# Second-stage transposes one more piece ahead, those of blocks 4 to 6 some chunks of look-ups later

## The chip, the cores and the metric

The kernel runs on one core of a Trainium2 chip. The time is the device time of one execution in microseconds (us), lower is better; times shown are medians over runs.

## What is computed

The reference is the interaction tower of a recommendation model. For each of 512 samples it looks up one 128-wide row in each of 26 tables, takes all pairwise dot products of these rows and of the rows with a dense vector, and sends the result through three layers:

```python
e = jnp.stack([tbl_f[ids[:, f]] for f in range(26)], axis=1)      # 512 x 26 x 128
sd = jnp.einsum('bfd,bd->bf', e, dense)
ss = jnp.einsum('bfd,bgd->bfg', e, e)
pairs = ss[:, iu, ju]                                             # f < g
h = concat([dense, sd, pairs, dense], axis=1)                     # 512 x 607
h = relu(h @ W_top1 + b_top1)                                     # 512
h = relu(h @ W_top2 + b_top2)                                     # 256
y = h @ W_top3
```

## The kernel before, in words

All arithmetic is in float32. The five engines run programs of their own, written out by hand; each is a fixed order of instructions with waits on counting semaphores, so the order in which the kernel's text issues work is the order of execution.

**Where the rows come from.** Ten of the tables have 1000 rows each. They are read whole, and TensorE picks their rows with one-hot matrices (line 342, "look-ups"). The other sixteen tables are gathered: GpSimd (POOL) issues 64 indirect DMAs (line 294), each of 128 rows of 512 bytes. Four of them make one block of 32 samples; there are 16 blocks, b0 to b15. The ring `rows` holds three blocks, so the gathers of block n wait until block n - 3 has been transposed by TensorE (semaphore `staged`), and POOL takes the blocks strictly in order.

**Look-ups.** Six groups g = 0 to 5 of one or two tables, with eight chunks k = 0 to 7 each. A chunk is two matmuls per table, and counts up `chunk_done`. VectorE makes the one-hot matrix of a chunk (line 552) into a ring of eight, so that of chunk m waits until chunk m - 8 is done; ScalarE moves a finished group into the tile `ET` (lines 480 and 482).

**Second-stage transposes.** A block is transposed by TensorE with four matmuls (line 325) into one of two PSUM banks `stage`, and ScalarE copies the bank into `ET` (line 470, `empty_stage`), which counts up `stage_taken`. Two banks mean that the transposes of a block wait until the block but one before them has been copied. Where they stand is set by three tables of names: `AMID` (behind chunk k of group g of the look-ups), `SOON` (directly behind the Gram matrices of piece p, ahead of that piece's layers) and `LATER` (behind the layers of piece p).

**Pieces.** The samples are then taken in nine pieces, p = 0 to 6 of 64 samples (two blocks) and p = 7 and 8 of 32. For each piece TensorE computes a Gram matrix per sample, 64 small matmuls of 27 columns in groups of four (line 371; the trace holds two records for each, 128 per piece of 64 samples), then the transposes of `SOON`, then the layers that are due for earlier pieces (lines 387, 398, 413, 415), then the transposes of `LATER`. The Gram matrices of piece p read blocks 2p and 2p + 1 (pieces 7 and 8: b14 and b15). VectorE and ScalarE move each Gram bank into the tile `Z` (lines 568 and 492), VectorE folds it (579, 586), and both take the first layer's output out of PSUM (591 and 501).

On TensorE the order behind the look-ups is `gram_piece(p)`, `SOON[p]`, `layers(p)`, `LATER[p]`. `layers(0)` and `layers(1)` are empty, `layers(2)` holds half of the first layer of 128 samples, and those from `layers(3)` on parts of both first layers.

Of the kernel before, what the change touches and what calls it, by code (L numbers as in the profile page):

```python
# [56 lines left out]
def layer1_of(p):  # L57

    return [((p - 2) // 2, c) for c in ((2, 3) if p % 2 else (0, 1))] if 2 <= p < NP - 1 else []
# [47 lines left out]
def dlrm_tower(nc, x, out):  # L107
    ctx = ExitStack()
    with ctx:
# [6 lines left out]
        def sem(name):  # L116
# [81 lines left out]


        AMID = {(0, 7): ["dense"], (1, 3): ["b0"], (2, 1): ["b1"], (2, 5): ["b2"], (3, 1): ["b3"],  # L200
                (3, 6): ["b4"], (4, 3): ["b5"], (4, 7): ["b6"], (5, 7): ["b7"]}

        SOON = {1: ["b8"], 2: ["b9"], 3: ["b10"], 4: ["b11"], 5: ["b12"]}
        LATER = {5: ["b13"], 6: ["b14"], 7: ["b15"]}
        STAGED = [s for g, k in sorted(AMID) for s in AMID[g, k]] + [s for n in range(NP) for s in SOON.get(n, []) + LATER.get(n, [])]

        def bank_of(name):
# [101 lines left out]
        def _(pe):  # L309
            def transposes(name):  # L310


                before, bank = STAGED.index(name), bank_of(name)
                if before >= 2:
                    pe.wait_ge(stage_taken, before - 1)
                if name == "dense":
                    pe.wait_ge(ident_ready, 1)
                    pe.wait_ge(dense_in, 16)
                    for t in range(T):
                        last = pe.transpose(bank[:, P * t:P * (t + 1)], dense_rows[:, t, :], ident[:, :])  # L320
                else:
                    n = int(name[1:])
                    pe.wait_ge(gathered[n], 16 * GB)
                    for k in range(GB):
                        last = pe.transpose(bank[:, P * k:P * (k + 1)], rows[:, (GB * n + k) % ROWS_RING, :], ident[:, :])  # L325
                last.then_inc(staged, 1)
# [37 lines left out]
            def gram_piece(p):  # L364

                gram_ready(p)
                b0, size = PIECES[p]
                for j in range(size // 4):
                    for i in range(4):
                        b = b0 + 4 * j + i  # L370
                        last = pe.matmul(gram[p % 2][32 * i:32 * i + 32, NV * j:NV * (j + 1)], ET[:, VP * b:VP * (b + 1)],  # L371
                                         ETv[:, b, 0:NV], start=True, stop=True)
                last.then_inc(gram_done, 1)
# [45 lines left out]
            def layers(p):  # L419

                for t, c in layer2_of(p):
                    layer2(t, c)
                for t, c in layer1_of(p):
                    layer1_dense(t, c)
                    layer1(t, c)
# [3 lines left out]
            for p in range(NP):  # L429
                gram_piece(p)  # L430
                for name in SOON.get(p, ()):
                    transposes(name)
                layers(p)
                for name in LATER.get(p, ()):
                    transposes(name)
# [13 lines left out]
        def _(act):  # L449
# [11 lines left out]
            def empty_stage(name):  # L461

                act.wait_ge(*filled(name))
                bank = bank_of(name)
                if name == "dense":
                    act.copy(denseT[:, :], bank[:, :])
                    act.copy(ETv[:, :, DENSE], bank[:, :]).then_inc(stage_taken, 1)
                else:
                    n = int(name[1:])
                    act.copy(ETv[:, BS * n:BS * (n + 1), 0:NM],  # L470
                             bank[:, :].rearrange("d (b v) -> d b v", v=NM)).then_inc(stage_taken, 1)
# [12 lines left out]
            def move_gram(p):  # L484
# [5 lines left out]
                for i in (2, 3):  # L490
                    for dst, src in z_moves(p, (i,)):
                        last = act.copy(dst, src)  # L492
                    if i == 2:
                        for name in SOON.get(p, ()):
                            empty_stage(name)
                last.then_inc(gram_act, 1)

            def take_odd(t, c):

                act.wait_ge(h1_done, HC * t + c + 1)  # L500
                act.activation(h1T[:, t % 2, c, :], layer1_bank(t, c), ACT.Relu, bias=b1c[:, c:c + 1]).then_inc(h1_odd, 1)  # L501
# [31 lines left out]
            for p in range(NP):  # L533
                move_gram(p)
                if layer1_of(p):
                    take_odd(*layer1_of(p)[1])
                for name in LATER.get(p, ()):
                    empty_stage(name)
# [152 lines left out]
```

## Time and profile before

| | |
|---|---|
| runs of the kernel before | 131.85, 132.18, 134.35 us |
| median | 132.18 us |
| the profiled execution's time | 132.72 us |
| its span in the trace | 130.9 us |
| TensorE busy | 94.0 us, 72% |
| VectorE, ScalarE, GpSimd busy | 73.7, 61.8, 67.5 us |
| granted TensorE clock, mean | 0.896 |

The span is the part of the execution that the trace covers; 1.8 us lie around it. The page of the profile gives busy times and, in 40 slices, how busy each engine was. The timeline lists an engine's instructions in order of time, merged where they follow each other without a gap, with the idle time before them and its inferred releaser in brackets. "issue" is idle time for which the profile shows no semaphore as the cause.

### The profile page before, as it was taken

To read this page: it belongs to the slowest core of one execution; us is meant where nothing else is said; L and a number is where in the kernel's file an instruction comes from. 1 tells how busy PE (TensorE), PEld (TensorE's weight loads), DVE (VectorE), ACT (ScalarE), POOL (GpSimd) and SP (SyncE) were. 2 spreads that over 40 slices of the span, in tenths; PEclk is the share of its full clock that TensorE was granted. 3 is DMA by queue.
4 is the path that set the end of the run, shared out by engine and by line. 5 is a ranking of instruction groups with operands and counts; after the bars stand their busy time and mean duration, and the time that the engine had idled before them with its cause. 6 is when DMAs were issued, how large, how long until landed. Compare 5 with 4: busy or idle time off the path is not lost.

```text
span 130.9 us, 3331 instructions
## 1 busy us (share of the span) xinstructions
PE 94.0 (72%) x1420; PEld 78.2 (60%) x1420; DVE 73.7 (56%) x170; ACT 61.8 (47%) x131; POOL 67.5 (52%) x70
## 2 busy tenths in 40 slices
PE   0089899999969999000547459397784997897892
PEld 0157688888858887000436349286674796786780
DVE  1387999999997835000008927264370731974621
ACT  3435591966908506300308909164370904964410
POOL 2878888787888787770831725538172560000000
PEclk9999999999999999965557756999999559999999
DMA  2999965947996121220110110102011110000000
GB/s 53 242 379 367 272 242 185 267 115 179 381 372 207 44 60 40 63 59 21 44 41 8 45 40 25 49 16 60 25 38 43 25 40 25 0 5 0 8 0 1
DMA packets 6849, 13.37 MB, mean 102 GB/s; under 512 B 2353, under 2 KB 3506, under 8 KB 6834
## 3 DMA queue, kind: packets, MB, share of 16 engines
q1 hardware_dynamic: 4112, 8.95, 21.4%
q0 software_dynamic: 2048, 4.20, 11.2%
q8 instruction: 11, 0.18, 0.6%
q10 hardware_dynamic: 674, 0.01, 0.3%
q14 instruction: 4, 0.03, 0.1%
HBM read 13.15 MB, written 0.00 MB: 100 GB/s over the span
## 4 chain that ended last, share of the span: by engine, by line
PE 44%; POOL 17%; issue 15%; DMA 7%; another core or an unknown queue 6%; ACT 6%; DVE 2%; DVEq 0%; ACTq 0%
POOL rows L294 17%; PE gram L371 12%; PE hidden L398 8%; PE second L415 6%; PE gram L342 6%; DMA rows<-in_tables_gather,idx 5%; PE stage L325 5%; PE hidden L387 3%; PE hidden L342 2%; ACT Z L492 2%; ACT ET L470 2%; ACT ET L482 2%; PE second L413 2%; DVE Z L568 2%
## 5 line engine op out<-in xcount | busy, mean ns | idle before, releaser
L294 POOL DMA_INDIRECT rows<-in_tables_gather,idx x64 | 66.8, 1044 | 39.0 <-issue 17.4
L568 DVE COPY Z<-gram 32x112 f32<-32x112 f32 (+3 forms) x72 | 23.0, 320 | 35.5 <-PE gram L371 34.6
L371 PE MATMUL gram<-ET 128*32 128x27 f32 x1024 | 17.0, 207 | 25.8 <-issue 12.8
L492 ACT COPY Z<-gram 32x112 f32<-32x112 f32 (+1 forms) x72 | 23.2, 322 | 23.7 <-PE gram L371 22.9
L371 PEld LDWEIGHTS gram<-ET 128*32 128x32 f32 x1024 | 14.1, 123 | 29.4 <-issue 26.0
L552 DVE TENSOR_SCALAR onehot<-ids,rowid 128x1024 fp32r<-128x1024 int16 (+1 forms) x48 | 28.7, 659 | 5.1 <-DMA ids<-in_ids_one 2.1
L342 PE MATMUL gram<-onehot,part 128*128 128x512 f32 x80 | 22.5, 434 | 6.6 <-DVE part L558 6.2
L342 PEld LDWEIGHTS gram<-onehot,part 128*128 128x128 f32 x80 | 16.4, 211 | 10.7 <-DVE onehot L552 6.2
L342 PE MATMUL hidden<-onehot,part 128*128 128x512 f32 x80 | 19.7, 397 | 0.6 <-issue 0.6
L342 PEld LDWEIGHTS hidden<-onehot,part 128*128 128x128 f32 x80 | 14.6, 188 | 3.7 <-issue 0.8
L558 DVE TENSOR_TENSOR part<-raw,part 128x1024 fp32r<-128x1024 f32 (+2 forms) x11 | 12.1, 1123 | 3.1 <-issue 2.4
L398 PE MATMUL hidden<-Z,W1s 128*128 128x128 f32 x84 | 13.2, 301 | 0.6 <-DVE Z L579 0.6
L398 PEld LDWEIGHTS hidden<-Z,W1s 128*128 128x128 f32 x84 | 12.2, 219 | 0.8 <-DVE Z L579 0.8
L459 ACT CAST part<-raw 128x1024 fp32r<-128x1024 f32 x9 | 9.4, 1070 | 5.2 <-DMA raw<-in_tables_one 4.3
L470 ACT COPY ET<-stage 128x512 f32<-128x512 f32 x16 | 9.5, 592 | 4.8 <-issue 4.6
L325 PE MATMUL stage<-ident,rows 128*128 128x128 f32 x64 | 10.8, 295 | 1.0 <-DMA rows<-in_tables_gather,idx 1.0
L415 PE MATMUL second<-W2s,h1T 128*128 128x256 f32 x32 | 10.2, 436 | 0.0
L325 PEld LDWEIGHTS stage<-ident,rows 128*128 128x128 f32 x64 | 8.0, 150 | 2.5 <-issue 1.4
L482 ACT COPY ET<-gram 128x512 f32<-128x512 f32 x5 | 5.3, 1145 | 6.9 <-PE hidden L342 5.6
L415 PEld LDWEIGHTS second<-W2s,h1T 128*128 128x128 f32 x32 | 5.8, 206 | 1.6 <-ACT h1T L501 0.4
L501 ACT ACTIVATE h1T<-hidden,b1c 128x128 f32<-128x128 f32 x7 | 2.6, 367 | 7.3 <-PE hidden L398 7.2
L387 PE MATMUL hidden<-denseT,W1e 128*128 128x128 f32 x28 | 6.0, 306 | 0.0
(38 smaller groups left out, 42.2 us busy)
## 6 DMA issues: line engine op xcount, KB each, us to landing
raw<-in_tables_one SPq DMA_DIRECT2D x9, 512.0 KB
ids<-in_ids_one SPq DMA_DIRECT2D x4, 256.0 KB, 5.5
rows<-in_tables_gather,idx POOLq DMA_INDIRECT x64
W1s<-in_W_pairs SPq DMA_DIRECT2D x1, 768.0 KB
W1d<-in_W_dense SPq DMA_DIRECT2D x1, 512.0 KB
W2s<-in_W_top SPq DMA_DIRECT2D x1, 512.0 KB
raw<-in_tables_one SPq DMA_DIRECT2D x1, 384.0 KB
ids<-in_ids_one SPq DMA_DIRECT2D x2, 128.0 KB, 3.6
```

The costliest lines, as they stand in the source:

```text
L294: pool.indirect_dma_start(out=rows[:, m % ROWS_RING, :], out_offset=None, in_=x["tables_gather"], in_offset=bass.IndirectOffsetOnAxis(ap=i ...
L325: last = pe.transpose(bank[:, P * k:P * (k + 1)], rows[:, (GB * n + k) % ROWS_RING, :], ident[:, :])
L342: last = pe.matmul(look_banks(g)[j], part[:, i % 4, n, D * k:D * (k + 1)], onehot[:, (KR * g + k) % RING, B * j:B * (j + 1)], start=(k == ...
L371: last = pe.matmul(gram[p % 2][32 * i:32 * i + 32, NV * j:NV * (j + 1)], ET[:, VP * b:VP * (b + 1)], ETv[:, b, 0:NV], start=True, stop=True)
L387: pe.matmul(layer1_bank(t, c), W1e[:, P * c:P * (c + 1)], denseT[:, P * t:P * (t + 1)], start=True, stop=False)
L398: last = pe.matmul(layer1_bank(t, c), W1s[:, s, P * c:P * (c + 1)], Z[:, t % ZT, s, :], start=False, stop=(s == 0))
L415: last = pe.matmul(at, h1T[:, t % 2, c, :], W2s[:, c, :], start=False, stop=(c == HC - 1))
L470: act.copy(ETv[:, BS * n:BS * (n + 1), 0:NM], bank[:, :].rearrange("d (b v) -> d b v", v=NM)).then_inc(stage_taken, 1)
L492: last = act.copy(dst, src)
L552: dve.tensor_scalar(onehot[:, m % RING, 0:w], ids16[:, B * SIDE[g][0]:B * SIDE[g][0] + w], rowid[:, k:k + 1], None, ALU.is_equal).then_inc ...
L558: return dve.tensor_tensor(part[:, i % 4, 1, cols], raw[:, i % RAW, cols], part[:, i % 4, 0, cols].bitcast(F32), ALU.subtract)
L568: last = dve.tensor_copy(dst, src)
```

## The change

Two tables of names change, and nothing else; no instruction is added or taken away.

```diff
         AMID = {(0, 7): ["dense"], (1, 3): ["b0"], (2, 1): ["b1"], (2, 5): ["b2"], (3, 1): ["b3"],
-                (3, 6): ["b4"], (4, 3): ["b5"], (4, 7): ["b6"], (5, 7): ["b7"]}
-
-        SOON = {1: ["b8"], 2: ["b9"], 3: ["b10"], 4: ["b11"], 5: ["b12"]}
-        LATER = {5: ["b13"], 6: ["b14"], 7: ["b15"]}
+                (4, 1): ["b4"], (4, 4): ["b5"], (5, 1): ["b6"], (5, 7): ["b7"]}
+
+        SOON = {p: [f"b{p + 8}"] for p in range(6)}
+        LATER = {6: ["b14"], 7: ["b15"]}
```

So b8 moves from behind piece 1 to behind piece 0, and so on up to b12, which moves from piece 5 to piece 4. b13 moves from behind the layers of piece 5 to ahead of them. In the look-ups b4 moves three chunks later, b5 one and b6 two; b7 stays. The gathers stand in the same order on GpSimd, but wait for transposes that stand elsewhere: those of b11 wait for b8, and so on to b15, which waits for b12.

On TensorE, at the first pieces behind the look-ups (`gram` is the bank of the Gram matrices, `stage` that of the transposes, and the number behind `gathered` is the block):

```order
 L371 MATMUL gram<-ET 32x27 [waits et_again,look_taken,stage_taken]
 L371 MATMUL gram<-ET 32x27 x63
+L325 MATMUL stage<-ident,rows 128x128 [waits gathered8,stage_taken]
+L325 MATMUL stage<-ident,rows 128x128 x3
 L371 MATMUL gram<-ET 32x27 [waits stage_taken]
 L371 MATMUL gram<-ET 32x27 x63
-L325 MATMUL stage<-ident,rows 128x128 [waits gathered8,stage_taken]
+L325 MATMUL stage<-ident,rows 128x128 [waits gathered9,stage_taken]
 L325 MATMUL stage<-ident,rows 128x128 x3
 L371 MATMUL gram<-ET 32x27 [waits gram_act,gram_dve,look_taken,stage_taken]
 L371 MATMUL gram<-ET 32x27 x63
```

The transposes of b8 now stand between the Gram matrices of pieces 0 and 1, and those of b9 where those of b8 stood.

On TensorE, at the end of the layers of piece 5, ahead of the Gram matrices of piece 6:

```order
 L387 MATMUL hidden<-denseT,W1e 128x128 [waits h1_odd]
 L398 MATMUL hidden<-Z,W1s 128x128 x3
-L325 MATMUL stage<-ident,rows 128x128 [waits gathered13,stage_taken]
-L325 MATMUL stage<-ident,rows 128x128 x3
 L371 MATMUL gram<-ET 32x27 [waits gram_dve,gram_act,stage_taken]
 L371 MATMUL gram<-ET 32x27 x63
```

The Gram matrices of piece 6 now follow the layers of piece 5 directly.

On TensorE, at the end of group 3 of the look-ups and the start of group 4:

```order
 L342 MATMUL hidden<-onehot,part 128x512 [waits onehot_ready]
 L342 MATMUL hidden<-onehot,part 128x512 x3
+L342 MATMUL hidden<-onehot,part 128x512 [waits onehot_ready]
+L342 MATMUL hidden<-onehot,part 128x512 x3
+L342 MATMUL gram<-onehot,part 128x512 [waits lo_ready,onehot_ready,look_taken]
+L342 MATMUL gram<-onehot,part 128x512
+L342 MATMUL gram<-onehot,part 128x512 [waits lo_ready]
+L342 MATMUL gram<-onehot,part 128x512
+L342 MATMUL gram<-onehot,part 128x512 [waits onehot_ready]
+L342 MATMUL gram<-onehot,part 128x512 x3
 L325 MATMUL stage<-ident,rows 128x128 [waits gathered4,stage_taken]
 L325 MATMUL stage<-ident,rows 128x128 x3
```

Three chunks that stood behind the transposes of b4 now stand ahead of them.

## Rows read from the trace of the kernel before

**Rows 1.** The page: TensorE's busy tenths and granted clock in 40 slices
```profile
PE   0089899999969999000547459397784997897892
PEclk9999999999999999965557756999999559999999
```
**Rows 2.** Chain that ended last, at the hole: start, us, what
```profile
53.65 8.20 another core or an unknown queue
...
61.87 0.38 ACT ET L480
```
**Rows 3.** Timeline of TensorE from 62 us: start, us, what, xcount, idle before
```profile
62.35 0.85 PE L371 MATMUL gram<-ET 128*32 128x27 f32 x46 [10.01 <-ACT ET L480]
67.84 2.72 PE L371 MATMUL gram<-ET 128*32 128x27 f32 x189 [1.12 <-issue]
70.49 0.65 PE L325 MATMUL stage<-ident,rows 128*128 128x128 f32 x4
72.09 0.87 PE L371 MATMUL gram<-ET 128*32 128x27 f32 x47 [0.95 <-ACT Z L492]
77.09 1.21 PE L371 MATMUL gram<-ET 128*32 128x27 f32 x71 [0.51 <-issue]
78.23 1.12 PE L325 MATMUL stage<-ident,rows 128*128 128x128 f32 x4
...
85.28 0.92 PE L371 MATMUL gram<-ET 128*32 128x27 f32 x82 [1.15 <-issue]
...
92.75 0.97 PE L371 MATMUL gram<-ET 128*32 128x27 f32 x89 [0.53 <-issue]
...
100.29 1.01 PE L371 MATMUL gram<-ET 128*32 128x27 f32 x87 [1.20 <-issue]
```
**Rows 4.** Timeline of GpSimd: gathers of b9 to b12 and b15, first or last
```profile
54.48 0.94 POOL L294 DMA_INDIRECT rows<-in_tables_gather,idx  x1 [0.30 <-issue]
...
62.17 0.94 POOL L294 DMA_INDIRECT rows<-in_tables_gather,idx  x1 [3.00 <-remote]
...
65.91 0.94 POOL L294 DMA_INDIRECT rows<-in_tables_gather,idx  x1 [0.31 <-issue]
71.41 0.94 POOL L294 DMA_INDIRECT rows<-in_tables_gather,idx  x1 [4.56 <-PE stage L325]
...
83.36 0.95 POOL L294 DMA_INDIRECT rows<-in_tables_gather,idx  x1 [0.30 <-issue]
...
106.37 0.94 POOL L294 DMA_INDIRECT rows<-in_tables_gather,idx  x1 [0.31 <-issue]
```
**Rows 5.** Chain that ended last: transposes of b9 to b13, a layer, piece 6
```profile
78.30 1.05 PE stage L325 x4
...
86.20 0.59 PE stage L325 x4
86.79 0.43 PE second L413 x2
...
89.39 0.67 PE hidden L398 x6
...
93.71 0.59 PE stage L325 x4
...
101.30 1.05 PE stage L325 x4
...
108.25 0.45 PE stage L325 x4
...
109.36 1.29 PE gram L371 x83
```
**Rows 6.** Timeline of TensorE in the look-ups: transposes of b4, group 5
```profile
38.49 0.63 PE L325 MATMUL stage<-ident,rows 128*128 128x128 f32 x4 [1.03 <-DMA rows<-in_tables_gather,idx]
...
47.98 3.92 PE L342 MATMUL hidden<-onehot,part 128*128 128x512 f32 x16
```
**Rows 7.** Timeline of VectorE: the last one-hot matrix
```profile
50.38 0.49 DVE L552 TENSOR_SCALAR onehot<-ids,rowid 128x512 fp32r<-128x512 int16 x1 [0.94 <-PE hidden L342]
```

## Prediction

> **What bounds the kernel now.** I read the page's slices first. TensorE is close to full up to about 52 us, then empty for three slices, and from 62 us on half busy with a pattern that repeats [rows 1]. So there are three stages, and the change touches the first and the last. Next the chain that ended last: through the hole it shows 8.20 us in which ScalarE waits for the end of the look-ups, with no releaser that the trace can name [rows 2]. Then the timelines of TensorE and GpSimd from 62 us on, laid side by side. The reader should see this in them: piece 0 starts at 62.35, issues 46 of its records in 0.85 us, and then crawls until 67.84, when the rest of pieces 0 and 1 goes through without a gap, 189 records in 2.72 us [rows 3]. The four gathers of b10 run from 62.17 to 66.85, which is 65.91 + 0.94 [rows 4]. The crawl ends 0.99 us behind them. Piece 2 does the same: 47 records, a crawl, and the rest from 77.09; b11's gathers start at 71.41 and take the same 4.68 us, so they end at 76.09, 1.00 earlier [rows 3, 4]. Piece 3 resumes at 85.28, and b12's gathers end at 84.31, 0.97 earlier [rows 3, 4]. Pieces 4 and 5 resume at 92.75 and 100.29 in the same way [rows 3]. Piece 6 meets no gather (the last one ends at 106.37 + 0.94 = 107.31, it starts at 109.36) and goes through in 1.29 us [rows 4, 5]. Piece 1 meets none either.
>
> So the last stage is bound by a loop that no share of busy time shows: transposes of block n let the gathers of block n + 3 go; while these run, the Gram matrices of the piece behind them stall once some 46 records have been issued; the stall ends about 1.0 us after the last gather; the rest of the piece and the next transposes follow. From the end of b9's transposes (78.30 + 1.05 = 79.35) to that of b10's (86.79) the loop takes 7.44 us, to b11's (94.30) 7.51, to b12's (102.35) 8.05 [rows 5]. The layers of each piece lie inside the loop, ahead of the Gram matrices, and are covered by the gathers.
>
> **The change part by part.** It moves transposes only; what counts is how many blocks of gathers a Gram piece has to sit out. Behind 62 us six blocks are still to be gathered, b10 to b15, in both kernels. Before, five of them stall a piece (0, 2, 3, 4, 5), and b15's run beside the layers of piece 5. After, b8's transposes stand behind piece 0, so b11's gathers start under piece 1, which ran free before, and b15's under piece 5: six pieces stall, 0 to 5.
>
> The sum, from the moment at which b7's transposes count as done, 61.85 (ScalarE's wait ends then, 53.65 + 8.20 [rows 2], and GpSimd's first gather follows at 62.17 [rows 4]):
>
> - Look-ups. b4's transposes waited 1.03 us for their gathers [rows 6]; three chunks later they find them landed, and all behind moves up 1.0. Whether the hole moves with it is unknown: VectorE's last one-hot matrix waits for the last chunk of group 4 and is released at 50.38 only, after 0.94 us of idling, although group 5 was running on TensorE from 47.98 on [rows 6, 7]. The counts arrive late, and the trace does not say why. Bounds: 0 gained if the hole's end is fixed by something else, 1.4 gained if one count fewer is queued, and 1.4 lost if b5's and b6's counts queue too. I take 1.0 gained, since the late counts follow chunks: start at 60.85. b5 and b6 move without cost: they sit between chunks either way, and the gathers of b8 and b9 that wait for them start after them still (b9's first at 54.48 [rows 4], well behind chunk 1 of group 5).
> - To b8's end: the stall of piece 0 ends at 67.84, 5.99 behind 61.85. In the chain the rest of piece 0 takes 1.10. b8's transposes now run in the low clock: 1.05 as b9's did [rows 5], where b8's took 0.65 [rows 3]. 5.99 + 1.10 + 1.05 = 8.14, so 68.99.
> - To b9's end, the new stall: 0.27 to the first gather (b8's end 71.14 to 71.41), 4.68 for four gathers, 1.0 to the end of the stall, the rest of the piece, 1.05 of transposes. Piece 1 starts together with the gathers and not 0.7 behind them as piece 2 did, so a little more of it is through; I take 0.9 for its rest, between 0.7 and the 1.21 of piece 2 [rows 3]. Together 7.9: 76.9.
> - To b10's end the same, piece 2 now: 7.9, bounds 7.44 and 8.2: 84.8.
> - To b11, b12 and b13: three turns of the loop with layers in it, as before. 7.44 + 7.51 + 7.6 (the third is 8.05 less the 0.46 by which transposes in the high clock are shorter [rows 5]) = 22.55: 107.35.
> - The layers of piece 5. In the high clock those of piece 3, which are the same instructions, took from 86.79 to 90.06 (89.39 + 0.67), 3.27 [rows 5]; before, piece 5's stood in a stretch in which the clock was granted at half (slices 32 and 33 [rows 1]) and took 5.90, from 102.35 to 108.25 [rows 5]. I take 3.27: 110.6.
> - Piece 6 follows at once. Before, b13's transposes and ScalarE's copy of them took 1.11, from 108.25 to 109.36 [rows 5]. That cost is gone, and is already left out of the sum.
>
> Piece 6 starts at 110.6 where it started at 109.36: 1.25 later. Behind it nothing changes. The profiled execution becomes 132.72 + 1.25 = 133.97, and since it lay 0.54 above the median, I expect 133.4. A stretch of half clock over piece 5's layers, as before, costs 0.46 + 2.63 more: 136.5.
>
> ScalarE's copies are hidden: b8's moves into its work on piece 0, b13's into that on piece 5, each 0.58 behind four moves out of the Gram bank, with the next user more than 2 us away.
>
> One rule against the trace. A piece under gathers loses over 4 us between its first 46 records and its rest [rows 3, 4]. The Trainium skill, page "SBUF — State Buffer", section "SBUF: two separate sides", says that DMA and TensorE use separate ports and cannot slow each other. By it the stall would have nothing to do with the gathers' data, moving them would cost nothing, and the sum would be rival C's, 130.1. What the trace shows is only that five stalls end within 0.97 to 1.04 us of the end of a block of gathers; it does not show by what way.
>
> **The rivals.**
> - A, my forecast: piece 1 stalls. For it: the 46 and 47 records that pieces 0 and 2 issue whatever the lead of the gathers (0.18 and 0.68 us). Something holds about that many ahead and is not refilled under gathers. Piece 1 has 128. Time 133.4, or with the half clock over the layers 136.5.
> - B: the gathers bite only once their data moves, and piece 1 is through by then (it lasts 1.3 to 1.55 us). Against it: piece 0 stalled at 63.20, 0.09 us after its first gather's issue ended. Then b9's end comes at about 71.5, the gathers of b11 and b12 run back to back (eight at 1.25 us from 69.3), piece 2 sits both out until 79.9, and b10 ends at 81.6 instead of 84.8: 3.2 less, 130.2, or 133.3 with the half clock.
> - C, the other side: the gaps belong to the pieces and not to the gathers, their ends a coincidence of two loops locked to each other. Then piece 1 stays free and every piece keeps its length; the change saves the 1.0 in the look-ups and the 1.11 ahead of piece 6: 132.18 - 2.1 = 130.1, and 127.0 if the half clock over piece 5's layers is gone too. It decides if piece 1 runs through under b11's gathers without a gap and piece 2 does not make up for it. Against it: five ends of five in step with the gathers, and pieces 1, 6, 7 and 8, without gathers, without a gap. The rule of the page above speaks for this one.
> - D: the hole grows, because the late counts queue behind those of b5 and b6: A plus up to 2.4, 135.8.
>
> **How the numbers follow.** A with the high clock over piece 5's layers 0.40, A with the low clock 0.28 (the page shows the low level in two stretches behind 56 us, one of them just there; a stretch starts in or behind a stall, and six stalls give it as many chances), B 0.14, C 0.13, D 0.05. The likeliest, 133.4, is the forecast. The range reaches from B and C to A with the low clock: 130.1 to 136.6. About 2% can be told from no change, so 129.5 to 134.8 is "the same". Faster: half of C where the clock gains too, 0.07. Slower: A with the low clock, D and a little of A by the bounds of its turns: 0.35. The rest, 0.58, is the same.
>
> **What would show it.** In the profile of the changed kernel: a gap inside piece 1's Gram matrices that ends about 1.0 us after b11's last gather; b15's gathers before the end of piece 5 and a gap there too; 7.4 to 8.2 us between the ends of transposes b8 to b13; no wait at b4's transposes, and the end of the hole near 60.9; piece 6 straight behind the layers of piece 5 at 110.6, or 113.7 in the low clock. If piece 1 has no gap, A is wrong. If the hole ends at 61.9 or later, the gain of the look-ups is not there.

## The result, and the profile after

The changed kernel took 137.18 us (median of 4 runs, 135.34 to 138.85), the kernel before beside it 132.3 us. The ratio of the two is 1.029, with an interval of 1.016 to 1.042 (it leaves out disturbed runs, and so lies below the 1.037 of the medians). In a second set of runs it was 1.039 (1.028 to 1.049). So the change makes the kernel some 3 to 4% slower. The forecast was 133.4 us with a range up to 136.6. The median lies 0.6 us above the range; the ratio times 132.18 us gives 136.0.

The profiled execution took 137.69 us, its span is 135.9. The page's slices of the changed kernel, TensorE and its granted clock:

```profile
PE   0089799999999991212394755929987799988893
PEclk9999999999999999755555555797799757999999
```

Against [rows 1] the half clock lasts longer: from slice 18 to 25 without a break, and again in slice 33, with 0.7 in the slices beside it. The timeline of TensorE in the changed kernel (start, us, what, xcount, idle before):

```profile
51.25 0.63 PE L325 MATMUL stage<-ident,rows 128*128 128x128 f32 x4 [0.39 <-issue]
56.69 0.63 PE L371 MATMUL gram<-ET 128*32 128x27 f32 x28 [4.80 <-issue]
...
67.49 1.39 PE L371 MATMUL gram<-ET 128*32 128x27 f32 x83 [0.50 <-issue]
68.81 1.12 PE L325 MATMUL stage<-ident,rows 128*128 128x128 f32 x4
69.85 1.22 PE L371 MATMUL gram<-ET 128*32 128x27 f32 x51
71.48 0.33 PE L371 MATMUL gram<-ET 128*32 128x27 f32 x4 [0.41 <-issue]
...
75.82 1.00 PE L371 MATMUL gram<-ET 128*32 128x27 f32 x56 [0.51 <-issue]
76.75 1.12 PE L325 MATMUL stage<-ident,rows 128*128 128x128 f32 x4
77.79 1.23 PE L371 MATMUL gram<-ET 128*32 128x27 f32 x51
...
83.77 1.04 PE L371 MATMUL gram<-ET 128*32 128x27 f32 x58 [1.10 <-issue]
```

Piece 1, which had no gap before [rows 3], issues 51 records from 69.85 on, crawls from 71.1 to 75.82, and issues its last 56 then. Piece 2 does the same 7.94 us later. GpSimd's timeline of the changed kernel shows b11's gathers, first and last:

```profile
70.19 0.94 POOL L294 DMA_INDIRECT rows<-in_tables_gather,idx  x1 [4.82 <-PE stage L325]
...
73.95 0.94 POOL L294 DMA_INDIRECT rows<-in_tables_gather,idx  x1 [0.30 <-issue]
```

They end at 74.89, 0.93 ahead of the end of the crawl. The chain that ended last, in the changed kernel, shows the ends of the transposes and the layers of piece 5 (those of before are [rows 5]):

```profile
68.87 1.05 PE stage L325 x4
...
76.81 1.05 PE stage L325 x4
...
84.81 1.05 PE stage L325 x4
...
92.62 0.59 PE stage L325 x4
...
100.04 0.59 PE stage L325 x4
...
107.65 1.05 PE stage L325 x4
108.69 0.72 PE second L413 x2
109.42 2.00 PE second L415 x4
...
114.41 1.22 PE gram L371 x82
```

Piece 6 starts at 114.41 where it started at 109.36: 5.05 later, and the span grew by 5.0. All of the loss lies ahead of piece 6, as forecast.

### The profile page after: what moved, and what is told of

Same layout as the page of the kernel before. It is cut to its first block, busy times and chain, and to the rows that moved or that the text cites. A ratio compares the mean times of both kernels' runs of the same rounds, so it can differ in the third digit from the quotient of the medians.

```text
span 135.9 us, 3331 instructions
## 1 busy us (share of the span) xinstructions
PE 99.5 (73%) x1420; PEld 81.4 (60%) x1420; DVE 73.5 (54%) x170; ACT 61.9 (46%) x131; POOL 67.7 (50%) x70
## 4 chain that ended last, share of the span: by engine, by line
PE 67%; issue 20%; DMA 5%; DVE 3%; ACT 2%; SPq 2%; DVEq 0%
PE gram L371 15%; PE hidden L342 14%; PE gram L342 11%; PE hidden L398 8%; PE stage L325 7%; PE second L415 7%; DMA raw<-in_tables_one 5%; PE hidden L387 3%; PE second L413 2%; ACT part L459 2%; DVE Z L568 1%; PE stage L398 1%; ACT ET L470 1%; SPq L258 1%; DVE onehot L552 1%
## 5 line engine op out<-in xcount | busy, mean ns | idle before, releaser
L371 PE MATMUL gram<-ET 128*32 128x27 f32 x1024 | 21.1, 211 | 25.2 <-issue 23.7
L371 PEld LDWEIGHTS gram<-ET 128*32 128x32 f32 x1024 | 16.3, 126 | 30.8 <-issue 28.5
L325 PE MATMUL stage<-ident,rows 128*128 128x128 f32 x64 | 11.8, 314 | 0.4 <-issue 0.4
L415 PE MATMUL second<-W2s,h1T 128*128 128x256 f32 x32 | 11.2, 469 | 0.0
L325 PEld LDWEIGHTS stage<-ident,rows 128*128 128x128 f32 x64 | 8.5, 159 | 2.0 <-issue 0.8
L415 PEld LDWEIGHTS second<-W2s,h1T 128*128 128x128 f32 x32 | 6.3, 223 | 1.8 <-issue 0.5
L482 ACT COPY ET<-hidden 128x512 f32<-128x512 f32 x4 | 4.2, 1174 | 5.5 <-PE hidden L342 5.5
```

Source lines behind the costliest of these rows:

```text
L415: last = pe.matmul(at, h1T[:, t % 2, c, :], W2s[:, c, :], start=False, stop=(c == HC - 1))
```

## The experiments

The kernel before took 131 to 134 us in some sets of runs and 107 to 111 us in others, and chip 8 showed both (109.4 us in one set, 132.0 us in a later one). Within one set it kept to one of the two. I call them the crawling and the quiet condition, after what their traces show below; no trace says what makes the difference. Each kernel is compared with the kernel before of its own set. Some kernels were run again because their first run had fallen in the quiet condition.

### Before and after once more

The kernel before again, for its trace: 

> The kernel before, unchanged, for its trace on the chip of the experiments, where it took 109.4 us and not 132.2. Theory G (on this chip no Gram piece crawls under gathers; GpSimd issues without a pause and its gathers' landing is what TensorE waits for): pieces 0 and 1 go through back to back without a gap, b8's transposes wait 1 to 2 us for their gathers, and GpSimd's gathers stand 1.25 us apart up to the last. Rival (the crawl is there too, shorter): gaps with releaser issue of over 1 us in at least three pieces.

It fell in the crawling condition, on chip 10: 133.21 us. Its timeline of TensorE:

```profile
52.31 0.55 PE L371 MATMUL gram<-ET 128*32 128x27 f32 x41
53.17 0.26 PE L371 MATMUL gram<-ET 128*32 128x27 f32 x4 [0.32 <-issue]
...
67.41 2.65 PE L371 MATMUL gram<-ET 128*32 128x27 f32 x178 [0.50 <-issue]
```

The theory for the quiet condition could not be tried here. But the trace shows that the hole of [rows 2] is no stage of its own. In this execution piece 0 starts at 52.31, right behind the look-ups, and crawls until 67.41: 15 us for its first 78 records, under the gathers of b8, b9 and b10, which run without a pause to 65.12. Whether piece 0 starts at 52.3 or at 62.35 [rows 3], its rest comes at 67.4 to 67.8.

The changed kernel again: 

> The changed kernel, unchanged, on the chip of the experiments. The two halves alone gave ratios 0.989 (look-ups) and 1.031 (pieces). Theory G: the halves add, ratio 1.015 to 1.025, with waits for gathers at b8's, b9's and b10's transposes of 6 to 8 us in all. Rival (the pieces' half costs more when the look-ups end earlier, since the gathers land no earlier): the look-ups' gain is eaten by longer waits, ratio 1.025 to 1.035, waits of 8 us or more.

Measured in the crawling condition: ratio 1.039 (1.028 to 1.049). Both expectations were for the other condition, so neither could be tried. Its trace (an execution of 136.98 us) has the same loop, with the end of b8's transposes at 69.16 and that of b13's at 107.35. Two rows of its chain that ended last, b13's transposes and piece 6:

```profile
106.71 0.64 PE stage L325 x4
...
113.50 1.42 PE gram L371 x94
```

From the end of b13's transposes to piece 6 it takes 6.15 us, the layers of piece 5.

### Each half alone

```diff
# look-ups' half: AMID of after, SOON and LATER of before
# pieces' half: AMID of before, SOON and LATER of after
```

The look-ups' half: 

> The look-ups' half of the change alone: b4, b5 and b6 later, the pieces as before. Theory A (the pieces' half costs, the look-ups' half gains a little): b4's transposes wait no more (1.03 us), but the end of b10's gathers moves up by some 0.4 us only, as in the changed kernel, where the rest of piece 0 started at 67.49 and not 67.84; time 0.3 to 1.0 us below before, ratio 0.992 to 0.998. Rival (the look-ups' half costs, because the counts of b5, b6 and b7 reach the other engines later): the rest of piece 0 starts later than 67.84 and the time is above before.

The pieces' half: 

> The pieces' half alone: b8 behind piece 0 and so on, the look-ups as before. Theory A (one more block of gathers sits inside a Gram piece): nearly the whole loss, ratio 1.025 to 1.045 (4 to 5.5 us), gaps in pieces 0 to 5, piece 6 starts at 114 to 115. Rival (the loss comes from the look-ups' half or from both together): ratio within 0.99 to 1.01.

Both fell in the quiet condition. The look-ups' half gave 0.989 (0.983 to 0.995), the pieces' half 1.031 (1.017 to 1.044). The repeat of the look-ups' half fell there too (chip 7): 

> The look-ups' half alone once more. On chip 8 it gave a ratio of 0.989. Where the pieces crawl, the start of the pieces is set by the end of b10's gathers (67.4 to 67.8 in the traces of before and after), and b4's missing wait of 1.03 us moves the start of b10's gathers only as far as b7's transposes move: theory A expects 0.990 to 1.000; rival (the look-ups' half carries part of the 1.03 to 1.04 that the whole change costs): 1.005 to 1.015.

It gave 0.997 (0.991 to 1.002). So in the quiet condition the look-ups' half gains between nothing and 1.7%, and the pieces' half is what costs. In the crawling condition neither half was timed alone. The way in which the pieces' half costs is another one here, and the gaps and the start of piece 6 that I had expected of it are not there. The pieces' half, quiet condition, timeline of TensorE:

```profile
52.27 1.83 PE L371 MATMUL gram<-ET 128*32 128x27 f32 x128
57.29 1.09 PE L325 MATMUL stage<-ident,rows 128*128 128x128 f32 x4 [3.19 <-DMA rows<-in_tables_gather,idx]
58.31 2.20 PE L371 MATMUL gram<-ET 128*32 128x27 f32 x128
61.65 1.08 PE L325 MATMUL stage<-ident,rows 128*128 128x128 f32 x4 [1.14 <-DMA rows<-in_tables_gather,idx]
62.66 2.03 PE L371 MATMUL gram<-ET 128*32 128x27 f32 x128
66.66 1.08 PE L325 MATMUL stage<-ident,rows 128*128 128x128 f32 x4 [1.97 <-DMA rows<-in_tables_gather,idx]
```

No piece crawls. TensorE reaches piece 0 with its clock high and finishes it in 1.83 us, and then waits 3.19, 1.14 and 1.97 us for b8, b9 and b10 to land. In the look-ups' half, where b8 stands behind piece 1, the same engine's timeline has

```profile
55.23 1.67 PE L371 MATMUL gram<-ET 128*32 128x27 f32 x109 [1.45 <-issue]
56.83 0.66 PE L325 MATMUL stage<-ident,rows 128*128 128x128 f32 x4
...
62.19 1.09 PE L325 MATMUL stage<-ident,rows 128*128 128x128 f32 x4 [1.66 <-DMA rows<-in_tables_gather,idx]
```

b8's transposes wait for nothing, and only b9's wait, 1.66 us. Its piece 6 starts at 84.26, that of the pieces' half at 86.56. In the quiet condition GpSimd issues one gather each 1.25 us with hardly a wait, so blocks land at a rate that TensorE can't hasten; asking for b8 to b10 one piece earlier turns into waiting. From b11 on the transposes wait for no gather in either trace.

### The gathers held back from piece 1

```diff
                 pool.wait_ge(*filled(...))
+                if n == 11 and k == 0:
+                    pool.wait_ge(gram_done, 2)
```

Tried three times. The first two fell in the quiet condition, where b11's gathers (from 64.09 on) come long after piece 1 anyway, so the added wait does nothing there. One run each gave 110.46 us beside 109.36 and 109.83 us beside 108.36: ratios 1.010 and 1.014. They stand in for the changed kernel itself, which was not timed in the quiet condition. Single runs of the kernel before reached 110.61 and 109.84 us in the same two sets, so what the whole change costs there is not clear of noise. The second and the third: 

> The changed kernel with b11's gathers held until piece 1's Gram matrices are done, once more, because the first try ran on chip 8, where no piece crawls. On a chip where they do (before takes 132 us): theory A: piece 1 goes through without a gap, 128 records in 1.3 to 1.6 us; b11's and b12's gathers run back to back and piece 2 crawls under all eight of them; b10's transposes end 1.5 to 3 us earlier than in the changed kernel there. Rival: piece 1 has a gap of 4 us all the same.

 

> The changed kernel with b11's gathers held until piece 1's Gram matrices are done, now timed. On a chip like chip 8, where no piece crawls, the held gathers come some 6 us after that moment anyway, so the kernel stands for the changed kernel itself: ratio to before 1.010 to 1.025. On a chip like chip 10 theory A expects that piece 1, if piece 0's rest starts at 67.4 to 67.8, goes through without a gap (128 records in 1.3 to 1.6 us), that piece 2 crawls under b11's and b12's eight gathers, and a ratio of 1.00 to 1.03, below that of the changed kernel there (1.039). Rival: piece 1 has its gap of 4 us all the same, and the ratio is 1.04 or more.

The third fell in the crawling condition, on chip 8. Its timeline of TensorE:

```profile
67.26 1.41 PE L373 MATMUL gram<-ET 128*32 128x27 f32 x85 [0.50 <-issue]
68.60 1.12 PE L327 MATMUL stage<-ident,rows 128*128 128x128 f32 x4
69.64 1.93 PE L373 MATMUL gram<-ET 128*32 128x27 f32 x128
71.50 0.78 PE L327 MATMUL stage<-ident,rows 128*128 128x128 f32 x4
72.46 0.85 PE L373 MATMUL gram<-ET 128*32 128x27 f32 x48 [0.17 <-issue]
...
83.78 0.85 PE L373 MATMUL gram<-ET 128*32 128x27 f32 x43 [0.50 <-issue]
84.56 1.12 PE L327 MATMUL stage<-ident,rows 128*128 128x128 f32 x4
```

and that of GpSimd, first and last of the eight gathers of b11 and b12:

```profile
72.38 1.09 POOL L296 DMA_INDIRECT rows<-in_tables_gather,idx  x1 [8.18 <-PE stage L327]
...
81.29 0.95 POOL L296 DMA_INDIRECT rows<-in_tables_gather,idx  x1 [0.31 <-issue]
```

Piece 1 goes through without a gap, 128 records in 1.93 us (granted clock 0.50; I had expected 1.3 to 1.6), at the same place in the program where it crawled in the changed kernel. That shows the cause of its crawl: the gathers that run beside it, and not its place. Piece 2 then crawls under all eight, up to 83.78. The ratio is 1.041 (1.034 to 1.049), no better than the changed kernel's 1.039, where I had expected 1.00 to 1.03. My expectation of 1.5 to 3 us gained at b10's transposes missed too: b10's transposes end at 85.7, in the changed kernel at 84.81 + 1.05 = 85.9. From b11's first gather to b10's end it takes 13.3 us here (72.38 to 85.68) and 15.7 in the changed kernel (70.19 to 85.86): 2.4 saved, but the gathers began 2.2 later. What piece 1 saves by missing its block of gathers, piece 2 pays.

### A longer ring

```diff
-ROWS_RING = 3 * GB
+ROWS_RING = 7 * GB
```

on top of the look-ups' half, so that the gathers hardly wait for transposes: 

> The look-ups' half of the change, pieces as before, and a ring for seven blocks in place of three, so that the gathers of block n wait for the transposes of block n - 7. Theory G (on this chip GpSimd never waits for the ring): nothing moves against the look-ups' half alone, ratio to before 0.985 to 0.995. Where a Gram piece crawls under gathers (the chip of the first runs, 132 us), theory A expects the gathers to run through and to end near 85 us, pieces 0 and 1 to crawl up to there, and the pieces behind them to go free: 4 to 8 us less than before.

Measured in the crawling condition: 143.74 us, ratio 1.085 (1.076 to 1.094). I expected 4 to 8 us less than before, and it was 11 us more. TensorE's timeline:

```profile
53.56 0.44 PE L371 MATMUL gram<-ET 128*32 128x27 f32 x28 [0.70 <-issue]
...
76.22 0.20 PE L371 MATMUL gram<-ET 128*32 128x27 f32 x1 [2.59 <-issue]
79.02 0.20 PE L371 MATMUL gram<-ET 128*32 128x27 f32 x1 [2.60 <-issue]
...
90.92 2.92 PE L371 MATMUL gram<-ET 128*32 128x27 f32 x200 [0.50 <-issue]
```

This trace is of the slowest of the five executions (146.43 us). GpSimd's last gather of the run without a pause, in its timeline:

```profile
84.59 0.95 POOL L294 DMA_INDIRECT rows<-in_tables_gather,idx  x1 [0.30 <-issue]
```

It ends at 85.54. Piece 0 crawls for 37 us, from 53.56 to 90.92, at times with one record in 2.8 us. So the crawl lasts as long as the gathers are let run, whatever the reason for which they run; it also gets slower with their number, and its tail, the time from the end of the last gather to the end of the crawl, grows: 0.93 us behind four gathers (changed kernel, b11), 2.3 behind the three blocks before 65.12 (before, second trace), 5.4 behind this run. That is why my expectation for this kernel failed. I had the gathers' end right (85), but not the tail, and only 28 records of piece 0 get done in the crawl, so that 200 records of pieces 0 and 1 stand behind it. And b15's gathers, which wait for b8's transposes even in this ring, run from 95.15 to 99.94 and make piece 2 crawl once more; only pieces 3 to 5 go free.

### Gathers left out, and plain DMAs in their place

```diff
-            for n in range(NB):
+            for n in range(10):
                 for k in range(GB):
                     gather(n, k)
```

> The changed kernel without the gathers of b10 to b15, and without TensorE's waits for them: these blocks are transposed from the rows that lie in the ring, so the results for samples 320 to 511 are not those of the reference, and 24 of 64 gathers are left out. Theory A: pieces 0 to 5 lose their gaps; the time from the first record of piece 0 to that of piece 6 falls from 57.6 us to 24 to 30 us, and with the end of b9's gathers near 59.5 us piece 0 goes through by 61 to 62; whole time 98 to 106 us. Rival (the gaps belong to TensorE's own issue): gaps of 3 us or more stay in at least three pieces and the time stays above 120 us.

And with the six blocks brought by plain DMAs from SyncE:

```diff
+            for n in range(10, NB):
+                sp.wait_ge(*filled(f"b{n - 3}"))
+                for k in range(GB):
+                    m = GB * n + k
+                    sp.dma_start(rows[:, m % ROWS_RING, :], x["tables_gather"][P * m:P * (m + 1), :]) ...
```

> The changed kernel with the gathers of b10 to b15 replaced by plain DMAs of the same size (128 rows of 512 bytes that lie one behind the other) issued from SyncE's queue behind the same waits: samples 320 to 511 are computed from other rows. The same bytes land in the same tiles. Where the pieces crawl: if the data in flight makes them crawl, gaps in pieces 1 to 5 stay, shorter since four transfers take less time. If GpSimd's making of the gathers does, there is no gap from piece 1 on and the time falls to within 2 us of the kernel that leaves them out.

Both (and the repeat of the first) fell in the quiet condition, one run each, so they say nothing of the crawl, and neither expectation on it could be tried. Leaving 24 of 64 gathers out brought 108.16 us beside 109.36 and 106.31 beside 108.36, a ratio of 0.989 and 0.981; the plain DMAs 107.87 beside 108.36. One thing is to be read from them. Piece 5's Gram matrices, in the pieces' half, in the repeat without late gathers, and with plain DMAs, each a row of TensorE's timeline:

```profile
80.92 1.85 PE L371 MATMUL gram<-ET 128*32 128x27 f32 x128
```
```profile
77.14 1.29 PE L372 MATMUL gram<-ET 128*32 128x27 f32 x128
```
```profile
78.33 1.29 PE L377 MATMUL gram<-ET 128*32 128x27 f32 x128
```

The granted clock was 1.00 over all three. In the windows of the last, data came in at 104 GB/s over that very piece (78.3 to 79.6); over the first, where gathers run, it was 53. So in the quiet condition too a Gram piece is slowed by GpSimd's gathers, by 0.56 us or 43%, and not by data in flight. The plain DMAs were not run in the crawling condition; that the same holds for the crawl is not shown. The rule that I had weighed (the Trainium skill, page "SBUF — State Buffer", section "SBUF: two separate sides": a DMA cannot be slowed by a compute operation nor the other way round) agrees with the plain DMAs' 1.29 us. It doesn't account for the 1.85 us under gathers. The crawl, which the longer ring and the held gathers tie to the gathers, goes against the reading that gathers cost TensorE nothing.

## Why the prediction was right, and where it was off

The change makes the kernel slower, where the prediction had put 0.58 on "the same" and 0.35 on "slower". The loop, the sixth stall and the new stall of piece 1 came as forecast; one term of the sum, the layers of piece 5, had the wrong size.

**Right: the bound.** The loop of gathers, crawl, rest and transposes sets the time up to piece 6, in both kernels, in the crawling condition. Two kernels show by intervention that the gathers hold the pieces back: gathers held until piece 1 was done freed piece 1, and gathers let run kept piece 0 back until 90.9.

**Right: the cost of the change.** One more block of gathers sits inside a Gram piece (six, where it was five) and the last one no longer lies beside the layers of piece 5. The turns of the loop came out as summed. In the changed kernel from b8's end to b9's 7.94 us (forecast 7.9), to b10's 8.00 (7.9), to b11's 7.35 (7.44), to b12's 7.42 (7.51). Why one piece ahead does not pay can be read from b15's first gather, before and after:

```profile
102.62 0.94 POOL L294 DMA_INDIRECT rows<-in_tables_gather,idx  x1 [3.36 <-PE stage L325]
```
```profile
100.90 0.94 POOL L294 DMA_INDIRECT rows<-in_tables_gather,idx  x1 [2.74 <-PE stage L325]
```

It started 0.27 behind b12's end in both, and only 1.72 earlier now. But behind b12's end stood only the layers of piece 5 before (5.90) and b13's transposes with their copy (1.11); now a whole turn with piece 5 in it (8.07) and then the layers (5.71). That is 8.07 - 1.11 - 0.19 = 6.77 more, less 1.72, and makes the 5.05 us.

**Off: the look-ups' term.** In the profiled execution this is what happened. I started the sum at 60.85, 1.0 earlier than before. b7's transposes were seen by ScalarE at 60.45, 1.4 earlier, the end that I had given for one count fewer. It did not help: the rest of piece 0 started at 67.49 and not at 66.84, only 0.35 earlier than in [rows 3]. The step of the sum that failed there is the stall of piece 0, "5.99 behind 61.85": it took 7.04, from 60.45 to 67.49. Its tail of 1.0 us holds for one block of gathers; here b9's and b10's ran almost back to back, and the tail was 67.49 less 65.38 = 2.1. And it left 83 records rather than 61 (189 less piece 1's 128): b8's end came 1.4 after the crawl's, not 1.1. Together b8's end lay at 69.92 where the sum had 68.99, 0.93 late. In the second trace of the changed kernel ScalarE saw b7's transposes at 61.35, only 0.5 earlier than before, the tail was 0.93, and b8's end lay at 69.16. From there the turns took 38.19 for my 38.36, and b13's end came at 107.35, where the sum had it. So this miss is one of the profiled execution more than of the kernel.

**Off: the clock.** The mis-sized term is "I take 3.27" for the layers of piece 5. I gave these layers in the high clock 0.40 and in the low clock 0.28, and took the high one. In the trace of the profiled execution they ran in the low clock, 108.70 to 114.41, 5.71 us for my 3.27, and the turn ahead of them took 8.07 for my 7.6. That is 2.9 us of the 3.8 by which piece 6 was later than forecast (114.41 for 110.6). In the second trace the layers took 6.15, and piece 6 started at 113.50; the alternative that I had named had 113.7, and 136.5 us for the whole. The second trace of before has half clock over the same layers (0.50 in its windows from 102.7 to 108.5), the second of after too (0.52 over 107 to 110, 0.51 to 114). So four traces of four of the two kernels in the crawling condition had it there, where I had read the one trace of before as one draw of two. A low clock that stood in the trace of before at the same place of the same loop was to be taken as part of the loop. The kernel with the held gathers had it for part of them (0.65 over 110 to 114). The kernel with the longer ring, whose pieces 3 to 5 meet no gathers, had them in the high clock (1.00 over 118.6 to 122.6).

**The rivals.** B is out: the crawl of piece 1 began at 71.1, before the second gather had started (71.44), and it lasted. C is out: the hold showed that the gaps do not belong to the pieces. D did not happen: the hole ended at 60.45 and 61.35 in the two traces, earlier than before, though late counts are real (below).

**What the prediction did not see:** that the same kernel takes 109 us in the other condition, with no crawl at all, and that its pieces' half costs there for another reason. My sum describes one of two regimes. In the quiet one the gathers of b8 to b10, at 1.25 us each, are the slower stream, and nothing that TensorE does earlier makes them land earlier. In the crawling one GpSimd itself waits for transposes, 2.7 to 4.8 us ahead of each block from b11 on in the changed kernel, and what costs is the sixth piece that sits out a block. No run shows a common cause behind the two.

No kernel that was timed in the crawling condition beats the kernel before. The look-ups' half alone is the best in the quiet one (0.989 and 0.997) of those that compute the whole result; in the crawling one it wasn't measured. There the rest of piece 0 starts 0.2 to 0.35 us earlier in the traces of the changed kernel than in those of before, which is an estimate of what it is worth.

## What to carry to other kernels

Ask of a work item that is issued ahead of its need which stream feeds it. Where that stream is already the slower one, one step ahead buys no earlier data, it only puts the wait, or the contention, in front of work that could have run. And where a gap in one engine ends about the same time behind another engine's burst, five times of five, take the burst for the likely cause: count how many pieces have to sit it out, before and after, and test it by holding the burst back once. Do not take that time for fixed: behind longer bursts it was 2.1 to 5.4 us where it had been 1.0.

## What the runs showed of the hardware that I had not expected

- TensorE's small matmuls (27 columns) nearly stop while GpSimd's indirect DMAs are in progress in the crawling condition: piece 0 in the ring kernel had 28 records in 0.44 us, and then single ones up to 2.8 us apart. Matmuls of 512 columns (from 20 us on) and the layers of 128 and 256 columns show no such gaps under the same gathers. By what way the gathers hold the small matmuls back stays open: the trace names no semaphore, and the small ones differ from the look-ups in pace too (128 records in 1.29 us without gathers, against 16 in 3.9 us), so that it is their size and not their number that counts is not shown.
- Counts that TensorE raises can reach other engines late. In the changed kernel b7's transposes stand at 51.25, Gram records of the next piece from 56.69 on, and ScalarE is let go for b7 at 60.45 only, 8.6 us behind the end of the transposes; its timeline:

```profile
56.22 1.06 ACT L480 COPY ET<-hidden 128x128 f32<-128x128 f32 x2 [5.11 <-remote]
60.45 0.58 ACT L470 COPY ET<-stage 128x512 f32<-128x512 f32 x1 [3.17 <-remote]
```

  The Gram records stand behind the transposes in TensorE's program, so these were issued by 56.69. The second trace of after has such a delay too (51.17 to 61.35). The second trace of before has none (ScalarE copies b7 at 52.69), and its time is the same as that of the first.
- The same chip ran the same kernel in 109.4 us in one set of runs and in 132.0 us in another. What set it is open. A profile of one set should not be taken for that of the chip.
